# A hybrid two-layer kernel: the order of statistics, scaling and score maxima in the last attention, and of the residual sums in retention

## What is computed

```python
phi_q = elu(rope(q)) + 1;  phi_k = elu(rope(k)) + 1
K = K * beta + phi_k                     # per head and decay, step by step in time
S = S * beta + phi_k * v
y = sum_m (phi_q . S) / (phi_q . K + eps) * mix
z = x + y @ Wout.T + bout                # x is the normalised input here
return layernorm(z) * ln_g + ln_b
```

```python
qkv = x @ W_qkv.T + b_qkv
probs = softmax(where(causal, q @ k.T, -inf) / sqrt(8))
return (probs @ v) @ W_o.T + b_o
```

## Time and profile before

| | |
|---|---|
| runs | 2304.18, 2304.64, 2307.56 us; median 2304.64 |
| profiled execution | 2307.55 us, its span 2305.8 us, mean PE clock 0.92 of full speed |
| busy share of the span | PE 87%, PE weight loads 65%, DVE 74%, ACT 44%, POOL 22% |
| retention | from 790 to 1098 us |
| last attention | from 1338 to 2064 us, with one exponential per step: 384 in all |
| costliest group | L2240, the reductions of the maxima: 608 of 659 ns on average |

### The profile page before, as it was taken

The page is one execution under the profiler, slowest core; times in us unless marked ns, Lnnn a source line. Parts: engine busy times, 40 slices in busy tenths (PEclk is TensorE's granted clock), DMA queues, the critical chain, the costliest instruction groups (busy, mean ns, idle before and its releaser), DMA issues. The chain is left out here.

```text
span 2305.8 us, 35920 instructions
## 1 busy us (share of the span) xinstructions
PE 1995.8 (87%) x12434; PEld 1494.9 (65%) x12434; DVE 1711.8 (74%) x5243; ACT 1018.6 (44%) x1596; POOL 509.3 (22%) x560
## 2 busy tenths in 40 slices
PE   5787799987999866663799978999999999979999
PEld 3454699976999733332699955565566556548998
DVE  6997788865888689997688766666666666627887
ACT  3442344433444332321444434565565565554443
POOL 1110100022000042320200024534433533320000
PEclk8998899998999886776899979999999999989999
DMA  3000100000000100000000000000000000000000
GB/s 96 6 5 4 53 1 1 2 1 1 2 1 1 39 1 0 1 1 0 1 1 1 1 1 1 1 1 1 1 1 1 1 1 1 1 1 6 11 10 15
DMA packets 17638, 15.75 MB, mean 7 GB/s; under 512 B 4209, under 2 KB 16177, under 8 KB 16946
## 3 DMA queue, kind: packets, MB, share of 16 engines
q1 hardware_dynamic: 15152, 12.66, 1.7%
q10 hardware_dynamic: 2306, 0.78, 0.2%
HBM read 10.55 MB, written 2.88 MB: 6 GB/s over the span
## 5 line engine op out<-in xcount | busy, mean ns | idle before, releaser
L2240 DVE TENSOR_REDUCE soft_mx<-psum 128x1 f32<-128x512 f32 (+3 forms) x608 | 382.3, 659 | 225.5 <-PE psum L2113 134.5
L2159 ACT ACTIVATE soft_prob<-psum 128x1024 f32<-128x1024 f32 (+3 forms) x384 | 306.6, 813 | 231.3 <-PE psum L2040 228.4
L2109 PE MATMUL psum<-soft_own,soft_stack 128*128 128x512 f32 (+3 forms) x768 | 249.1, 383 | 31.5 <-DVE soft_mx L2240 28.9
L2040 PE MATMUL psum<-soft_stack,soft_own 128*128 128x512 f32 (+3 forms) x768 | 231.4, 385 | 3.0 <-POOL soft_stack L2015 2.3
L2040 PEld LDWEIGHTS psum<-soft_stack,soft_own 128*128 128x128 f32 x768 | 123.2, 192 | 137.6 <-issue 92.0
L2109 PEld LDWEIGHTS psum<-soft_own,soft_stack 128*128 128x128 f32 x768 | 140.6, 194 | 88.1 <-DVE soft_mx L2240 71.1
L2057 PE MATMUL psum<-soft_prob,soft_v_pad 128*32 128x512 f32 (+3 forms) x1536 | 167.1, 507 | 7.3 <-POOL soft_prob L2021 6.1
L1056 DVE SCALAR_TENSOR_TENSOR x<-psum,ffn0b_cw,x 128x128 f32<-128x128 f32 x512 | 144.2, 344 | 29.9 <-PE psum L934 21.4
L1056 DVE SCALAR_TENSOR_TENSOR x<-psum,ffn1b_cw,x 128x128 f32<-128x128 f32 x512 | 144.1, 344 | 30.0 <-PE psum L934 21.2
L1056 DVE SCALAR_TENSOR_TENSOR x<-psum,ffn1a_cw,x 128x128 f32<-128x128 f32 x512 | 144.2, 344 | 29.8 <-PE psum L934 20.9
L1056 DVE SCALAR_TENSOR_TENSOR x<-psum,ffn0a_cw,x 128x128 f32<-128x128 f32 x512 | 144.2, 344 | 29.6 <-PE psum L934 21.1
(11 more groups left out here) (435 smaller groups left out, 3871.6 us busy)
## 6 DMA issues: line engine op xcount, KB each, us to landing
s_ffn_w<-in_ffn_w SPq DMA_DIRECT2D x4, 1024.0 KB, 7.8
out_x<-x SPq DMA_DIRECT2D x8, 256.0 KB, 2.3
x<-in_x SPq DMA_DIRECT2D x4, 384.0 KB, 7.5
mamba_coef_dram<-mamba_out_coef SPq DMA_DIRECT2D x8, 96.0 KB, 1.6
s_ret_w<-in_ret_w SPq DMA_DIRECT2D x1, 640.0 KB, 3.5
x<-in_x SPq DMA_DIRECT2D x4, 128.0 KB, 3.3
s_ret_cos<-in_ret_cos SPq DMA_DIRECT2D x1, 512.0 KB, 4.4
s_ret_sin<-in_ret_sin SPq DMA_DIRECT2D x1, 512.0 KB, 5.2
```

The costliest lines, as they stand in the source:

```text
L2040: ins = pe.matmul(e_ps[:, n % 2, j, low(n):BLK], own[:, u % 3, 2 * pair + j, kt * P:(kt + 1) * P], stack[:, u % HT, qb * BLK + low(n):(qb ...
L2109: ins = pe.matmul(per_head[:, n, :], stack[:, u % HT, i * P:(i + 1) * P], own[:, u % 3, g, half * BLK:half * BLK + width], start=(n == 0), ...
L2159: nc.scalar.activation(prob[:, done % PROBS, :, low(n):BLK], e_ps[:, n % 2, :, low(n):BLK], ACT.Exp, scale=float(HD) ** -0.5).then_inc(exp ...
L2240: nc.vector.tensor_reduce(mx[:, i, half, heads.start:heads.stop], bank[:, 0:width * len(heads)].rearrange("p (g k) -> p g k", k=width), AX ...
```

## The change

In retention, `keep(a)` waits from block 2 on also for `phi_ready` of the count `a`, that is for `phi` of block `a - 1`, and in POOL's order it comes behind `z_power`. VectorE's `scans` is cut in two functions: `states` (the five scans) and `products`. In block 0 `rope(1)` moves between them and `statistics(2)` behind the products; in the other blocks the order is the same.

In the last attention the event `stat` is cut in `stat` (statistics; the power on POOL) and `scale` (scaling; on POOL the sum with the output bias), which comes at once in the opening and three steps later in units 1, 5 and 9. In the opening `("v", 1)` and the first key stack of unit 1 come ahead of `("sh", 0, 0)`. In unit 0 the other stacks and own rows of unit 1 come earlier and the bias sums one step later; six maxima of unit 1 lie around `("sh", 0, 1)` in step 7, the other 32 two to a step behind it. In units 1 to 14 odd steps and steps 0, 8 and 16 get two maxima each, the other even steps one (step 23 gets one as well).

```diff
--- before.py
+++ after.py
@@ -1424,6 +1424,8 @@
             def keep(a):
 
                 pool.wait_ge(norm.xn_ready, a + 1)
+                if a >= 2:
+                    pool.wait_ge(phi_ready, a)
                 if a >= KEPT:
                     pool.wait_ge(z_ready, a - KEPT + 1)
                 row = [P, GT, P]
@@ -1450,10 +1452,10 @@
                     invert(i + 2)
                 if i + 1 < BLOCKS:
                     rotate(i + 1)
+                if i:
+                    z_power(i - 1)
                 if i + 2 < BLOCKS:
                     keep(i + 2)
-                if i:
-                    z_power(i - 1)
             z_power(BLOCKS - 1)
 
         @block.tensor
@@ -1690,7 +1692,7 @@
                                             phi[:, p, 1, :].unsqueeze(1).to_broadcast([P, 2, BLK]), ALU.mult)\
                         .then_inc(ring_used, 1)
 
-            def scans(q, m):
+            def states(q, m):
                 p, n = q % 2, DECAYS * q + m
                 dve.wait_ge(clipped, q + 1)
                 dve.wait_ge(ring_used, products_up_to(PAIRS * (q + 1) - 1))
@@ -1701,6 +1703,9 @@
                         state[:, m, s, :], beta[:, p, m, :], phi[:, p, 1, :] if s == 0 else kv[:, p, s - 1, :],
                         state[:, m, s, BLK - 1:BLK] if p else 0.0, ALU.mult, ALU.add)
                 ins.then_inc(scanned, 1)
+
+            def products(q, m):
+                p, n = q % 2, DECAYS * q + m
                 dve.wait_ge(scanned, n + 1)
                 if n:
                     dve.wait_ge(num_ready, n)
@@ -1754,18 +1759,24 @@
             rope(0)
             features(0)
             for i in range(BLOCKS):
-                if i + 2 < BLOCKS:
-                    statistics(i + 2)
-                if i + 1 < BLOCKS:
-                    rope(i + 1)
                 if i:
+                    if i + 2 < BLOCKS:
+                        statistics(i + 2)
+                    if i + 1 < BLOCKS:
+                        rope(i + 1)
                     divide(i - 1)
-                scans(i, 0)
+                states(i, 0)
+                if i == 0:
+                    rope(1)
+                products(i, 0)
+                if i == 0:
+                    statistics(2)
                 if i:
                     add_residual(i - 1)
                 if i + 1 < BLOCKS:
                     features(i + 1)
-                scans(i, 1)
+                states(i, 1)
+                products(i, 1)
                 if i:
                     finish(i - 1)
                 invert(i)
@@ -1821,10 +1832,10 @@
     def maxima(a, b):
         return [("m", 0, j) for j in range(a, b)]
 
-    start = [("stat", 0), ("pad", 0), ("xt", 0), ("stat", 1), ("qk", 0, 1), ("qk", 0, 0)]
+    start = [("stat", 0), ("scale", 0), ("pad", 0), ("xt", 0), ("stat", 1), ("scale", 1), ("qk", 0, 1), ("qk", 0, 0)]
     start += [first[0], ("own", 0, 0), ("v", 0), first[1]]
     start += [("xt", 1)] + maxima(0, 4) + [("qk", 1, 1)] + maxima(4, 8) + [("qk", 1, 0)] + maxima(8, M_FIRST)
-    start += [first[2], ("sh", 0, 0), first[3], ("own", 0, 1)]
+    start += [first[2], ("v", 1), second[0], ("sh", 0, 0), first[3], ("own", 0, 1)]
     units = []
     for u in range(UNITS):
         b, t = divmod(u, HT)
@@ -1838,17 +1849,19 @@
             late = M_JOBS - M_FIRST
             for j in range(late):
                 at[j * FIRST_STEPS // late].append(("m", 0, M_FIRST + j))
-            for j in range(M_JOBS):
-                at[FIRST_STEPS + j * (E_STEPS - FIRST_STEPS) // M_JOBS].append(("m", 1, j))
-            put((1, ("v", 1)), *zip((2, 3, 5, 6), second), (3, ("own", 1, 0)), (6, ("own", 1, 1)))
-            put((4, ("bias", 0)), (5, ("bias", 1)), (FIRST_STEPS - 1, ("sh", 0, 1)))
+            at[FIRST_STEPS - 1] += [("m", 1, j) for j in range(3)] + [("sh", 0, 1)] + [("m", 1, j) for j in range(3, 6)]
+            for j in range(6, M_JOBS):
+                at[FIRST_STEPS + (j - 6) * (E_STEPS - FIRST_STEPS) // (M_JOBS - 6)].append(("m", 1, j))
+            put(*zip((1, 3, 4), second[1:]), (1, ("own", 1, 0)), (4, ("own", 1, 1)))
+            put((5, ("bias", 0)), (6, ("bias", 1)))
             put((9, ("oev", 0, 0)), *zip((10, 11, 13, 14), stack_events(0, 2)), (12, ("otr", 0, 0)), (15, ("sh", 1, 0)),
                 (12, ("own", 2, 0)), (16, ("own", 2, 1)), *zip((17, 18, 20, 21), stack_events(0, 3)), (19, ("pad", 1)))
             units.append(at)
             continue
         if u < UNITS - 1:
+            slots = [n for n in range(E_STEPS) for _ in range(2 if n % 2 or n % 8 == 0 else 1)]
             for j in range(M_JOBS):
-                at[j * E_STEPS // M_JOBS].append(("m", u + 1, j))
+                at[slots[j * len(slots) // M_JOBS]].append(("m", u + 1, j))
         put((1, ("sh", u, 1)))
         put((1, ("oev", u - 1, 1)), (3, ("otr", u - 1, 1)))
         put((9, ("oev", u, 0)), (12, ("otr", u, 0)))
@@ -1859,8 +1872,9 @@
         if b < BATCH - 1:
             q = BPB * (b + 1)
             if t == 1:
-                put((2, ("stat", q)), (6, ("xt", q)), (8, ("qk", q, 0)), (10, ("qk", q, 1)), (12, ("stat", q + 1)),
-                    (16, ("v", q)), (17, ("xt", q + 1)), (19, ("qk", q + 1, 0)), (21, ("qk", q + 1, 1)))
+                put((2, ("stat", q)), (5, ("scale", q)), (6, ("xt", q)), (8, ("qk", q, 0)), (10, ("qk", q, 1)),
+                    (12, ("stat", q + 1)), (15, ("scale", q + 1)), (16, ("v", q)), (17, ("xt", q + 1)),
+                    (19, ("qk", q + 1, 0)), (21, ("qk", q + 1, 1)))
             if t == 2:
                 put(*zip((6, 8, 10, 15), stack_events(b + 1, 0)), (17, ("v", q + 1)))
             if t == 3:
@@ -1996,7 +2010,7 @@
                         own_rows(nc.gpsimd, u, p, own_ready)
                 if kind == "stat":
                     norm.invert(pool, at[0])
-                if kind == "bias" or kind == "stat" and at[0] >= BPB:
+                if kind == "bias" or kind == "scale" and at[0] >= BPB:
                     q, = at
                     pool.wait_ge(norm.xn_ready, q + 1)
                     tiles = x[:, q * GT:(q + 1) * GT, :]
@@ -2210,6 +2224,8 @@
                     norm.statistics(dve, q)
                     if q == 0:
                         nc.vector.memset(neg[:, :, :, :], 0.0).then_inc(pads_set, 1)
+                if kind == "scale":
+                    q, = at
                     dve.wait_ge(norm.rstd_ready, q + 1)
                     if q:
                         dve.wait_ge(misc_ready, place["xt", q - 1] + 1)
```

## The result

The changed kernel takes 2270.26 us in the median of four runs (2265.08 to 2271.54); beside it the kernel before took 2305.15 (four runs). The ratio is 0.984, with a 95% interval from 0.983 to 0.985: 34.9 us less. The forecast was 2264, its range 2250 to 2285.

What follows compares the result with a forecast made beforehand. VectorE's queue was taken to bound retention, PE's idle time and granted clock the last attention. Terms -5.8 - 12.0 - 7.9 - 10.5 - 4.0 = -40.2 us gave 2264 us against the runs' median of 2304.64; range 2250 to 2285.

Steps and rivals of the forecast that it cites:

- Units 1, 5, 9: Last attention: scaling three steps after statistics cuts PE's idle time, -12.0 us, and restores the clock, -7.9 us.
- The clock follows the pauses: Last attention: PE's pauses bring its clock to 1.2 GHz, costing 0.45 us per microsecond there; without them it returns.
- the rival that it doesn't: Clock drops are not the pauses' doing, so -7.9, -4.5 and -1.0 fall away: 2278 us; chance 0.10.
- Half the stalls move: Units 1, 5, 9: two shorter blocks per statistics each still stop PE, half the gain stays away: 2274 us; chance 0.09.
- First group: Attention's opening and unit 0: work moved into pauses at both shifts, with the clock, -10.5 us, bounds 0 and -16.
- The six maxima and the thinner steps behind them: Unit 0: maxima around the second shift fill its pauses, -1.7 us; two a step afterwards instead of 2.4, -1.8 us.
- The first pause: First shift: v(1) and one key stack fill PE's pause, -1.5 us.
- Retention, steady blocks: Residual sums run beside the keys' products instead of the scans: 1.7 us per block, -8.6 us over five.
- Retention, block 0: VectorE's new order delays `phi(1)` by 2.5 us, and the residual sums' overhang adds 0.3: +2.8 us.
- The rival that retention returns nothing: POOL is released too late, or block 0 loses 8 us: 2270 us; chance 0.06.
- Slots: Other attention units: one maximum at most even steps, two at odd ones, cuts PE's waits: -4 us, bounds -10 and +8.
- The slower rival: Odd steps' second maximum waits for its bank in 168 places, 0.55 us each, losing 92 us: 2356 us; chance 0.04.

Runs made afterwards that it cites:

- e8: Changed kernel without the residual sums' added wait for `phi` in retention, new order kept: 2272.53 us.
- e3: Changed kernel with scaling put back at the same step as the statistics in units 1, 5 and 9: 2289.21 us.
- e12: Changed kernel with one to eight idle VectorE reductions added behind each of the six statistics of units 1, 5 and 9: 2288.89 us.
- e7: Changed kernel with `statistics(2)` back ahead of the first scans in retention's block 0, `rope(1)` left between scans and products: 2266.58 us.
- e9: Changed kernel with VectorE's old order in retention's block 0, and POOL's own rows waiting for the first half's negative maxima: 2259.00 us, ratio 0.980 to before.
- e4: Changed kernel with the maxima of units 1 to 14 spread evenly by the old formula: 2272.76 us.

## Why the prediction was right, point by point

- **Sum and median.** In the two stages the sum was -40.2 us, measured -39.7. The median gained 34.9. That the stages agree to half a microsecond is in part luck: the executions profiled were the slowest of before and the fastest of after, and `e8`, the same kernel but for one wait, needs 3.6 us more in the attention. The forecast subtracted from a median what was read on one profiled execution; the spread of retention's start (6 us) and of the opening (3 us) are of the same order as the gap of 6.3 us between 2264 and 2270.26. Shown is only that kernels with the same code in a stretch differ so; where the other three runs of after lost their time was not profiled. The clock alone does not tell: one of them, 2270.76 us, had the same mean clock, 0.929, as the fastest.
- **Units 1, 5, 9:** -12.0 for idle time and -7.9 for the clock, measured -20.0 together. PE idles 1.3 us in each, near unit 2's 1.2. `e3` undoes it with 19.3. This was the best founded step, because the same execution had units with and without the stall. One side effect was missed: GpSimd's bias sum, moved with the scaling, now runs beside the first half of `neg` (L2270) in these units, which takes 0.77 instead of 0.18 us.
- **The clock follows the pauses.** For units 1, 5 and 9 this is shown, and the rival that it doesn't (2278) falls by `e3` and `e12`. At the second shift it is not: "If PE stays busy there, the 10.1 us at 1.2 GHz return" came true in five of eleven executions, and in `e7` all of the 10.2 us stayed. What brings the clock down there without a pause is open. The price of 0.45 us per microsecond at 1.2 GHz came out as 0.43 in `e3`; in unit 13, with 3.4 us at that level in some executions and 6.8 in others, it is 0.19 to 0.27.
- **Half the stalls move** (2274): no. The scaling alone, three steps later, leaves idle time at 1.3 us.
- **First group:** -10.5, measured -9.5 in a stretch that scatters by 3. The six maxima and the thinner steps behind them, -1.7 - 1.8 = -3.5, came out as -3.9 to -4.6. The first pause, -1.5, was worth 0.5 to 0.8; why not more is not shown. The clock, -4.5 - 1.0 = -5.5, is not a fixed sum: the time at 1.2 GHz was 23.9 and 13.7 us with the plan of before, 6.8 to 15.8 with that of after. Between before and after, as profiled, it fell by 17.1 us; between other pairs it would not fall at all.
- **Retention, steady blocks:** -8.6 (five times 1.7 is 8.5), measured -8.8, by the mechanism named: an operation of VectorE with an operand in PSUM doesn't contend, so sums beside the keys' products cost nothing. The prediction gave the wait for `phi` as what places them; `e8` shows that the order behind `z_power` does.
- **Retention, block 0:** +2.8, measured +2.0. Sign and size were right as a comparison with before, but the step took the loss as the price of the rest. `e9` shows that it buys nothing: without it the second `phi` comes 4.3 us earlier. The rival that retention returns nothing falls.
- **Slots:** -4.0, measured -3.2 (table above; -4.5 by `e4`), and right for the wrong reason. The step that failed is "such pairs exist in either pattern": the slots gave -6.0 in nine units alone, and 0.6 each in units 1, 5, 9. And it looked for its loss in bank waits only, not in what the shifted reductions bring `neg` to lie beside. In unit 13 that was the own rows, and cost 3.8. The slower rival (a bank wait in 168 places) did not occur.

What missed was thus one mechanism, not in the list at all though its pieces were: the earlier trace rows show sums and scans slowing each other. I applied that to retention and did not ask it of the attention, where GpSimd has operations of 3.6 us. Two errors of the prediction, the slots' gain put too low and this loss left out, came close to cancelling.

## What to carry to other kernels

Cut a piece that waits for another engine in two and put the second half where its input is long done: here that made half of the gain in the two stages, a good part of it clock that PE's stops had cost. Before accepting a new order, list every short VectorE operation on SBUF on the path to PE, and what GpSimd runs at that time: `neg`, starting a tenth of a microsecond behind a long GpSimd operation, waited for all the rest of it. Operations with two SBUF operands come first, but the clip of `e7` had only one. When a change has several edits in one place, undo each alone; the order of block 0 lay hidden behind a gain more than twice its cost.

## What the runs showed of the hardware

- VectorE's 128x16 operation with two SBUF operands: 0.185 us at the shortest, 0.192 in the median, 3.536 behind a GpSimd product of 3.60 us that began 0.1 us earlier. Whether it hits is a matter of some tenths of a microsecond: 0.34 us ahead of the product it took 0.41 us.
- It goes both ways: two GpSimd sums took 5.00 instead of 2.5 us beside VectorE's products (`e7`), and the scans 6.61 instead of 4.54 (`e9`).
- A VectorE operation that reads a single SBUF tensor can be hit too: the clip of `beta` took 1.69 instead of 0.69 us (`e7`), the first half of `neg` 0.77 instead of 0.18 (after). The keys' products, with one operand from PSUM, kept their 2.35 us beside the residual sums.
- PE's clock fell after pauses of 1.75 us in most places, after none of 1.27 or 1.30 us in `e12`, and in or behind those of 2.86 or 2.87 us in unit 13 in all eight executions that have them. It also fell where PE had no pause above 0.77 us, at the second shift in six of eleven executions. A microsecond at 1.2 GHz cost 0.43 us between two units of `e3`, 0.19 to 0.27 in unit 13, and 0.24 to 0.41 in the opening and first unit. Which pause is followed by it differs from execution to execution of the same code, and with it the time.
